# Recurrence of a hybrid block: two of the four selected copies of r at level 16 move from ScalarE to GpSimd

## The reference, cut to what matters

```
def step(state, rkvw):
    r_t, k_t, v_t, w_t = rkvw
    a = k_t[..., :, None] * v_t[..., None, :]
    y = jnp.einsum('bhk,bhkv->bhv', r_t, state + u[None, :, :, None] * a)
    new_state = w_t[..., :, None] * state + a
    return (new_state, y)
```

## Time and profile before

| | us |
|---|---|
| median of 3 runs | 1362.44 (1359.52 to 1365.13) |
| span of the profiled execution, first to last instruction | 1357.2 |
| PE / DVE / ACT / POOL busy over the span | 1148.5 / 926.0 / 613.3 / 551.3 |
| the recurrence's eight chunks, roughly | 590 to 1080 of the span |
| one chunk, start to start | about 60 |

### The profile page before, as it was taken

How to read it: one execution, slowest core, us unless ns; L and a number is a source line. 1 busy time by engine, 2 the same in 40 slices (tenths; PEclk the granted TensorE clock), 3 DMA queues, 4 the chain that set the end, 5 groups by cost and what they waited for, 6 DMA issues and landing times. The chain is left out here.

```text
span 1357.2 us, 34954 instructions
## 1 busy us (share of the span) xinstructions
PE 1148.5 (85%) x14041; PEld 820.0 (60%) x14041; DVE 926.0 (68%) x1959; ACT 613.3 (45%) x1310; POOL 551.3 (41%) x537
## 2 busy tenths in 40 slices
PE   7999999976599999478999898898996658999970
PEld 4677777754488888235555555555554437888860
DVE  4778787757765656568678695968756376565646
ACT  2334343313255555144737455474635233555544
POOL 3333333202377776324151432415141115777750
PEclk9999999978699999698999999999999778999995
DMA  8032222108743332200000001000000095333338
GB/s 302 24 126 93 81 90 83 64 1 296 248 169 104 103 105 90 75 31 3 33 3 33 24 12 33 3 33 4 1 3 2 18 389 166 103 104 101 104 101 345
DMA packets 50683, 125.66 MB, mean 93 GB/s; under 512 B 7649, under 2 KB 26977, under 8 KB 47713
## 3 DMA queue, kind: packets, MB, share of 16 engines
q1 hardware_dynamic: 36896, 86.20, 17.7%
q0 software_dynamic: 13632, 37.24, 8.7%
HBM read 79.63 MB, written 43.78 MB: 91 GB/s over the span
## 5 line engine op out<-in xcount | busy, mean ns | idle before, releaser
L1090 POOL DMA_INDIRECT ffn_xs<-xn_rows,ffn_from_row x142 | 137.6, 969 | 123.7 <-DVE ffn_second_y_at L1472 81.0
L1098 POOL DMA_INDIRECT y_rows<-ffn_ys,ffn_to_row x142 | 140.1, 987 | 55.1 <-issue 35.4
L1253 PE MATMUL ffn_ps_h<-ffn_w_high,ffn_xst 128*128 x568 | 155.3, 396 | 0.6 <-issue 0.6
L1500 DVE TENSOR_TENSOR ffn_act_in<-ffn_silu_g,ffn_ps_h 128x256 f32<-128x256 f32 x142 | 59.9, 422 | 139.0 <-ACT ffn_silu_g L1132 139.0
L1132 ACT ACTIVATE ffn_silu_g<-ffn_ps_h 128x256 f32<-128x256 f32 x142 | 54.8, 386 | 144.3 <-PE ffn_ps_h L1253 144.3
L1273 PE MATMUL ffn_ps_o<-ffn_w,ffn_act_t 128*128 x284 | 117.2, 435 | 0.5 <-DVE ffn_act_t L1505 0.5
L1253 PEld LDWEIGHTS ffn_ps_h<-ffn_w_high,ffn_xst 128*128 128x128 f32 x568 | 97.4, 190 | 18.2 <-issue 1.1
L1833 POOL TENSOR_TENSOR rec_mixed_w<-rec_mixed_w,rec_xnt 128x512 f32<-128x512 f32 x16 | 17.2, 1091 | 207.5 <-DVE rec_mixed_w L2634 207.5
L1253 PE MATMUL ffn_ps_h<-ffn_w_low,ffn_xst 128*128 x284 | 89.8, 398 | 0.0
L644 DVE TENSOR_TENSOR ret_probs<-ret_score,ret_causal 128x2048 f32<-128x2048 f32 x32 | 73.3, 2292 | 18.7 <-PE ret_score L485 18.7
L1275 PE MATMUL ffn_ps_o<-ffn_w,ffn_act_t 128*128 x284 | 79.2, 279 | 0.0
(11 more groups left out here) (353 smaller groups left out, 2894.8 us busy)
## 6 DMA issues: line engine op xcount, KB each, us to landing
home<-y_rows SPq DMA_DIRECT2D x30, 512.0 KB, 5.0
w_split<-home SPq DMA_DIRECT2D x24, 512.0 KB, 4.1
ffn_w_high<-w_split SPq DMA_DIRECT2D x8, 1024.0 KB, 8.8
ffn_w_low<-w_split SPq DMA_DIRECT2D x8, 1024.0 KB, 10.7
ffn_w<-w_split SPq DMA_DIRECT2D x8, 1024.0 KB, 14.4
home<-in_f_w SPq DMA_DIRECT2D x12, 512.0 KB, 6.1
xn_rows<-home SPq DMA_DIRECT2D x12, 512.0 KB, 11.7
out<-x SPq DMA_DIRECT2D x8, 512.0 KB, 5.7
```

The source lines that it names most:

```text
L1090: pool.indirect_dma_start(xs[:, n % SLOTS, :], None, xn_rows[:], bass.IndirectOffsetOnAxis(ap=from_row[:, n:n + 1], axis=0)) \
L1098: pool.indirect_dma_start(y_rows[:], bass.IndirectOffsetOnAxis(ap=to_row[:, m:m + 1], axis=0), ys[:, m % SLOTS, :], None).then_inc(ys_stor ...
L1253: mm = pe.matmul(ps_h[:, u % 2, :], one_pass(xst[:, u % 2, part, k, :]), one_pass(w1[w_part][k][:, bass.ds(e, E_COLUMNS)]), start=(part + ...
L1500: dve.tensor_tensor(act_in[:, u % 2, :], silu_g[:, u % 2, :], ps_h[:, u % 2, FF:2 * FF], ALU.mult) \
```

## The change

POOL gets a function `r16_shared_out(c)`, called after `carry(n)`, that waits for R16 and makes the copies e = 2 and 3 of level 16 as `tensor_scalar` by `one_of`, counted on a new semaphore. ACT makes e = 0 and 1 only. The waits of PE (`scores_by_16`) and DVE (`r_to_32`) for the copies become two waits, and the counts of `r_parted` are lowered by two per chunk.

```diff
+        r16_shared = sem("r16_shared")
...
-        PARTS = 3 * HEADS
+        SHARED = HEADS // 2
+        PARTS = 3 * HEADS - SHARED
...
+                def r16_shared_out(c):
+                    pool.wait_ge(chain, c * CHAIN + R16)
+                    if c >= 1:
+                        pool.wait_ge(score_in_psum, c * CT)
+                    for e in range(HEADS - SHARED, HEADS):
+                        pool.tensor_scalar(r_16p[:, :, e, :, :], r[:].rearrange("p k (b two i) -> p k b two i", two=2, i=16)[:, :, :, 1, :],
+                                           one_of[:, e:e + 1], None, ALU.mult).then_inc(r16_shared, 1)
...
                     if now:
                         carry(n)
+                        r16_shared_out(n)
...
-                def parted(into, source):
-                    for e in range(HEADS):
+                def parted(into, source, heads=HEADS):
+                    for e in range(heads):
...
                 def r16_parted(c):
                     act.wait_ge(chain, c * CHAIN + R16)
-                    parted(lambda e: r_16p[:, :, e, :, :], r[:].rearrange("p k (b two i) -> p k b two i", two=2, i=16)[:, :, :, 1, :])
+                    parted(lambda e: r_16p[:, :, e, :, :], r[:].rearrange("p k (b two i) -> p k b two i", two=2, i=16)[:, :, :, 1, :],
+                           heads=HEADS - SHARED)
...
                 def scores_by_16(c, i):
                     pe.wait_ge(k_copied, c * COPIES + K16_REST)
-                    pe.wait_ge(r_parted, c * PARTS + 2 * HEADS)
+                    pe.wait_ge(r_parted, c * PARTS + 2 * HEADS - SHARED)
+                    pe.wait_ge(r16_shared, (c + 1) * SHARED)
...
                 def r_to_32(c):
-                    dve.wait_ge(r_parted, c * PARTS + 2 * HEADS)
+                    dve.wait_ge(r_parted, c * PARTS + 2 * HEADS - SHARED)
+                    dve.wait_ge(r16_shared, (c + 1) * SHARED)
                     raise_r(c, 16)
```

## The result

The changed kernel takes 1371.84 us (median of 8, 1366.86 to 1375.65) beside 1363.67 for the kernel before (8 runs on the same chip, 1359.52 to 1367.47): ratio 1.0067, 95% interval 1.0041 to 1.0093. It is slower by 8.2 us by the medians and by about 9 by the ratio, whose interval is 5.6 to 12.7 us. The ratios in this document are those on record and not quotients of the medians; the two differ by up to 0.3%. The device time of a run lies 1.8 us above its span (1368.29 and 1366.5 for the profiled run), so the profiled execution of before took about 1359.0. Of the 5.3 us between its span and the median of the runs, 1.8 are this difference, and the rest is that it was one of the quicker executions.

What follows compares the result with a forecast made beforehand. PE was taken to bound the kernel, through its wait before scores_by_32(n, 0). The chunks' shifts of R32 summed to +3.25 us on 1362.44, giving 1365.7 us, range 1358 to 1374.

Steps and rivals of the forecast that it cites:

- The bound: PE's 0.60 us wait before scores_by_32(n, 0), traced to R32 waiting 0.35 for level 16's last copy; shifts pass one to one.
- same: Verdict on the whole kernel: +3.25 us lies within about 0.5% (6.8 us), what a measurement can tell; leaning slow.
- my own signs of being right: After R16: second L2737 about D + 0.5, DVE not waiting at R32, R32 about 0.5 later, PE's wait about 1.1.
- rival 1: At R16, POOL's copies run beside DVE as meant: gain 2.9 us, 1359.5; pair L2737 stays at 0.87; chance 0.15.
- rival 2: POOL's tensor_scalar at R16 is slow in runs of 16 elements, over 1.5 us: +23 us, 1385; chance 0.12.
- What POOL's copy costs: Duration of one POOL tensor_scalar copy of level 16, from neighbouring instructions: 0.85 us, range 0.58 to 1.27.
- D: Assumed time of one POOL copy of level 16 after R16: 0.85 us, range 0.58 to 1.27.
- What it does to DVE: After R16, POOL's first copy holds DVE's second L2737: slip 0.94 us, R32 +0.52 in n = 1, 2, 3, 5.
- turn-taking: DVE instructions with two SBUF operands and POOL sums each stand still for the whole of the other; applied to POOL's copies.
- the 9.9 of D = 1.27: Upper bound with POOL's copy at 1.27 us: the second copy reaches DVE's decay products, +9.9 us over the chunks.
- the 23 of D = 2.1: Slow POOL copies of 2.1 us after R16, DVE's work behind them: +3.0 us in n = 2, 23 us over the chunks.
- The added waits at nothing: 32 added waits on PE and 8 on DVE: taken as 0, at most 0.05 us each, 1.6 us in all.

Runs made afterwards that it cites:

- Late copies: Kernel before, POOL untouched, ACT making copies e = 0 and 1 of level 16 a second time, PE and DVE waiting for all six: ratio 1.0147.
- Side copies: Kernel before plus two POOL tensor_scalar at R16 that read constants and write a free tile, nobody waiting for them at R32: ratio 1.0010.
- the products: Changed kernel with POOL's two copies made as tensor_tensor products of two SBUF inputs in place of tensor_scalar: ratio 1.0032 to the kernel before.
- waits only: Changed kernel's semaphores and waits, but ACT makes all four copies of level 16 and POOL none: ratio 1.0009 to the kernel before.

## Why the prediction was right, and where it was wrong

- The bound was read rightly: the copies are last by 0.35, R32 is chained to PE's wait at `scores_by_32(n, 0)` and to mask(n, 0), and a shift of R32 comes back as PE's wait one to one (0.60 to 1.70 for +1.11). Late copies show it without POOL.
- The direction and the range were right, 1371.84 measured in 1358 to 1374. The size was not: +3.25 worked out, 8 to 9 measured, beyond the 0.5% that I called "same". Some 1.2 us of the distance from 1365.7 are the kernel before, whose eight runs have 1363.67 where the three that I started from had 1362.44.
- That the range held is luck in part. Of my own signs of being right, two are missing: the second L2737 isn't lengthened, and DVE does wait for the copies at R32. In their place stand a sign of rival 1 (the pair at 0.87) and that of rival 2 (POOL's instruction over 1.5 us).
- The step "What POOL's copy costs" failed first: D = 0.85, at most 1.27, taken from the two-input sum with one input taken away. It is 1.56 at best and up to 2.05 beside DVE. One input fewer isn't cheaper: the product of two inputs in the same place takes 1.04 to 1.22. The Trainium skill's 769 ns for 512 elements (GPSIMD Engine Reference, 3.1) isn't reached here either.
- The step "What it does to DVE" failed second. I took the turn-taking of the earlier trace rows over to `tensor_scalar`, with DVE as the one that stands: a slip of 0.94 by a held L2737. Side copies and the changed kernel show 0.87 to 0.88 there in chunks 1 to 5, so the slip is 0. The contention falls on POOL, whose copies stretch to 2.05 and 1.91, and DVE pays for it in one piece, as a plain wait of 1.45 for the second copy. Only in chunk 0 is DVE held, by 0.44.
- The rule of the Trainium skill (SBUF — State Buffer, "Who interferes with whom"), by which a DVE instruction with two SBUF inputs and a GpSimd instruction that reads SBUF hold each other, is borne out in that they do contend. That the second is blocked for the whole of the first holds nearly for POOL's instructions of two inputs (R32 in n = 7, the products) and not for `tensor_scalar`: 0.44 of a copy of 1.73, 0.65 of one of 2.21. The measurement decides.
- The two errors pull apart: with D = 1.56 and DVE held, the sum would have been about 14, between the 9.9 of D = 1.27 and the 23 of D = 2.1, and the time some 1376.7, above the range. It didn't come, because `tensor_scalar` hardly holds DVE.
- By chunk (R32 against the kernel before, worked out and measured): n = 1, 2, 3 and 5 +0.52 and +1.10; n = 4 +0.9 and +0.85 from the chunk's start (+1.5 from R16); n = 0 -0.6 and -0.7; n = 6 -0.3 and +0.4; n = 7 +1.15 and +1.56 at the copies of level 32, there by `add_near_1` moved behind the copies and holding R32, as foreseen in kind. Measured they add up to 6.5, worked out to 3.25. (The terms for D = 1.27 add up to 9.8, not 9.9.)
- The sum has no term for the granted clock. Half clock stands behind the longer gap in chunk 3; how much of the 2 to 3 us between 6.5 and the measured 8 to 9 is the clock's isn't shown.
- The added waits at nothing: borne out (1.0009, R32 0.07 later).

## What to carry to other kernels

When a share of work moves to a slower engine, what counts is when its last piece lands, not what is freed: here two copies of 1.6 to 2 us behind a start that was the same as ACT's were 1.45 late, one was 0.5 early. Split by the time of the last piece, one to POOL for three to ACT. That took the loss away (0.9981, inside its interval); a gain could be told once only, with a copy of level 32 moved as well (0.9956, and 0.9978 on another chip). And take the duration of an operation that the trace doesn't show from no neighbour of another kind without a wide upper end: fewer inputs isn't less time on POOL.

## What the runs showed of the hardware that wasn't expected

- POOL's `tensor_scalar` with a per-partition scale, 512 fp32 elements in runs of 16, takes 1556 ns at best, its `tensor_tensor` with a broadcast second input over the same elements 1037 to 1218 ns.
- What a POOL instruction does to DVE's instructions with two SBUF inputs depends on its kind here. A `tensor_scalar` of 512 elements held DVE for 0.44 us of its 1.73 in chunk 0, one of 768 for 0.65 of 2.21. POOL's instructions of two inputs held it nearly to their end: the product of 512 for 0.79 of 1.21, the sum of 768 for 1.45 of 1.72 (R32 in n = 7). For each element read that is 0.85, 0.85, 0.77 and 0.94 ns; that the hold is POOL's reading is a guess that these numbers allow, and no run varied the size on purpose.
- In most chunks it is POOL that pays: its copy takes 2.05 in place of 1.56 beside a DVE pair that isn't lengthened, with the same order and distance of starts as in chunk 0.
- The changed kernel, with PE's gap at 1.70 for 0.60, has a mean granted clock of 0.96 in chunks 0 to 6 of its profile (before 0.99, waits only 0.97, side copies 0.98). Filling the gap with transposes brought the clock to 0.98 and didn't bring the time back.
